# A two-mixer block: xn's transposition, the order of the sums on VectorE, the second tile's row sums, and the norm's root on GpSimd are moved

## The chip, the cores and the metric

The kernel runs on one core of a Trainium2 chip. A core has TensorE (matrix products, written PE, its weight loads PEld), VectorE (DVE), ScalarE (ACT), GpSimd (POOL) and SyncE (SP, which issues DMA transfers). The metric is device time in microseconds (us) from start to end of one execution; lower is better.

## The reference

All data are float32. The input x has shape (4, 1024, 512), 4096 tokens of 512. Four layers follow each other, each with a layer norm ahead and its input added behind:

```python
x = x + attn_a(layernorm(x))   # mixer A: 16 heads of 64, state 64
x = x + ffn(layernorm(x))
x = x + attn_b(layernorm(x))   # mixer B: 64 heads of 16, state 128
x = x + ffn(layernorm(x))
```

A mixer projects the normed input to a gate z (1024 columns), a part xBC, and dt (one column for each head); it runs a causal convolution of four taps over xBC and a SiLU, splits it into x, B and C, and then computes, token by token,

```python
state = state * dA_t + einsum(dtx_t, B_t)
y_t   = einsum(C_t, state)
y     = y + D * x
```

with dt = softplus(dt + dt_bias), dA = exp(dt * A). y is gated with silu(z), normed by its root mean square (in A the gate comes before the norm, in B behind it), and projected back to 512 columns. The feed-forward layer works on a gate for each token and one message for each sequence; the change doesn't touch it.

## The kernel before

The program runs the stages A, F, B, F, one after the other. A mixer stage works on supertiles of 256 tokens, 16 of them, and a supertile has two tiles of 128 tokens, j = 0 and 1. Supertile 0 and the last two are written out, the 13 between run in a hardware loop. The recurrence is done in chunks of one tile: within a tile by products with a matrix of decays (seg, decay, ydiag), between tiles by a state that is carried along (yoff reads it, state0 and state1 add to it).

Each engine runs an order of its own, and they meet in semaphores. TensorE's order is written by `schedule` and `head` as a list of step names. While supertile i is finished, the projections of supertile i + 1 are put between its steps: dt and the blocks blk0, blk1, ... (9 in A, 10 in B) in the first tile's half, z0, z1, z2 in the second's, and z's last quarter, zz, at the start of the next head. The names that matter here:

- zz, z0 to z2, blk, dt: projections with w_in, line 527 (dt at 556). They read xnT.
- xnT0, xnT1: transposition of the normed input xn of supertile i + 1 (line 551), copied by ScalarE (`xnT_copy`, line 738).
- xT0 to xT3, BG (A) or BT, GT (B): transpositions of the convolved x and B, and B times C (lines 571, 576, 533).
- prs, prt, pout: for the last tile of the supertile before, the sums of squares (line 625), the column of them (629), and the projection with w_out (633). rs0, rt0 and out0 are the same for tile 0 of this supertile. VectorE copies the sums (`square_sums`, 1121), forms the variance (`rms_var`, 1125), scales (`out_scale`, 95 to 97) and adds the projection to the residual (`out_add`, 1135).
- yoff0a, yoff0b, yoff1a, yoff1b: products with the state (604 in A, 606 in B), taken by VectorE's `from_state` (1079) into y1. GpSimd then adds the skip part (1291), forms xw from xdt (1302 in A, 1298 in B), and decays the state (1308).
- small0, small1: row sums of the two tiles (595), taken by `small_sums` on VectorE (1049, 1050), from which `exponent_sides` (1059 to 1064) makes the operands of seg.
- make_xdt (1023 in A, 1018 in B): x times dt. slot_mult (1090): the product with gt that makes decay ready for ydiag; two slots a tile in A, eight in B.
- norm_stats, norm_rsqrt and norm_apply: the layer norm of the supertile after the next: statistics on VectorE (928 to 933), the root as exp(-0.5 ln v) on ScalarE (733, 734), refined by one Newton step on VectorE (`newton_rsqrt`, 87 to 90), and applied (940).

All steps that are not seg, ydiag or ident use one of two banks of PSUM, work[0] and work[1], in turns. A step therefore waits until the step two places ahead of it in the list has been taken out of its bank; `freed` says by whom. That is the rule by which an order on one engine becomes a wait on another:

```python
if idx >= 2:
    freed(pe, sec.uses[idx - 2], i, n)
```

For instance, in the head the transposition xnT1 is two places ahead of dt, and pout two places ahead of blk0; pout's bank is free once `out_add` is done.

Of the kernel before, what the change touches and what calls it, by code (L numbers as in the profile page):

```python
# [11 lines left out]
P = 128  # L12
# [72 lines left out]
def newton_rsqrt(dve, nc, link, r, v, tmp):  # L85

    link(nc.vector.tensor_tensor(tmp, r, r, ALU.mult))
    link(nc.vector.tensor_tensor(tmp, tmp, v, ALU.mult))
    link(nc.vector.tensor_scalar(tmp, tmp, -0.5, 1.5, ALU.mult, ALU.add))
    link(nc.vector.tensor_tensor(r, r, tmp, ALU.mult))  # L90


# [7 lines left out]
def build_constants(nc, ctx, ffn):  # L100
# [9 lines left out]
    c["mean_w"] = sb("mean_w", [P, P])  # L110
    c["ident_bf"] = sb("ident_bf", [P, P], BF16)
# [22 lines left out]
    with nc.Block() as block:  # L134
# [12 lines left out]
        def _(pool):  # L147
# [49 lines left out]
def mixer_phase(nc, sig, before, cfg, c, first_mixer, psum, x_src, x_dst, w):  # L197
# [19 lines left out]
    with ctx:  # L217
# [16 lines left out]
        ln_v, ln_r, ln_t = sb("ln_v", [P, 2]), sb("ln_r", [P, 2]), sb("ln_t", [P, 2])  # L234
# [108 lines left out]
        def head(prev, nxt):  # L343
            return (["zz", "xT0", "xT1", "xT2", "xT3"] + b_and_g + ["seg0.0"] + (["prs"] if prev else [])
                    + ["yoff0a", "yoff0b"] + (["prt"] if prev else [])
                    + (["xnT0", "xnT1"] if nxt else []) + (["pout"] if prev else []))

        def schedule(prev, nxt):

            steps = head(prev, nxt)  # L350
            for p in range(NP):
                steps += fill0[2 * p] if nxt else []
                steps += [f"seg0.{p + 1}"] if p + 1 < NP else ["small1"]
# [116 lines left out]
        with nc.Block() as block:  # L470
# [252 lines left out]
            def _(act):  # L723
# [6 lines left out]
                def norm_rsqrt(m):  # L730

                    act.wait_ge(var_ready, m + 1)
                    link(nc.scalar.activation(ln_r[:], ln_v[:], ACT.Ln))
                    nc.scalar.activation(ln_r[:], ln_r[:], ACT.Exp, scale=-0.5).then_inc(r0_ready, 1)

# [98 lines left out]
                def supertile(sec, prev, nxt):  # L834
                    i = sec.i
                    z_copy(sec, "zz")
                    for k in range(4):
                        xt_copy(sec, k)
# [8 lines left out]
                    if nxt:  # L847
                        xnT_copy(sec, 0)
                        xnT_copy(sec, 1)
# [14 lines left out]
                    for p in range(NP):  # L864
# [5 lines left out]
                        if p == 0 and sec.ln is not None:  # L870
                            norm_rsqrt(sec.ln)
# [17 lines left out]
                norm_rsqrt(0)  # L889
# [11 lines left out]
                norm_rsqrt(1)  # L901
# [3 lines left out]
                per = 4  # L905
# [13 lines left out]
            def _(dve):  # L919
# [15 lines left out]
                def norm_apply(n):  # L935
                    dve.wait_ge(r0_ready, n + 1)
                    newton_rsqrt(dve, nc, link, ln_r[:], ln_v[:], ln_t[:])
# [201 lines left out]
                def supertile(sec, prev, nxt):  # L1139
                    i = sec.i  # L1140
                    masked_gt(sec)
                    make_xdt(sec, 0)
# [10 lines left out]
                    if prev:  # L1153
                        out_add(sec, "pout", i - 1, 1)
                    for p in range(NP):
                        for g in (2 * p, 2 * p + 1):
# [11 lines left out]
                            elif g % 2 == 0:  # L1168
                                small_sums(sec, 1)
# [70 lines left out]
                per = 2 + 3 + 3 + 2 + 2 * NB + 2 * 4  # L1240
# [15 lines left out]
            def _(pool):  # L1256
# [7 lines left out]
                def tile_steps(i, j):  # L1264
# [36 lines left out]
                    else:  # L1301
# [628 lines left out]
```

## Time and profile before

| | us |
|---|---|
| median of three runs | 3284.08 |
| lowest, highest | 3274.63, 3286.74 |
| the profiled execution | 3287.7 |
| its span | 3286.0 |
| TensorE busy | 2902.2 |
| VectorE busy | 2016.2 |
| ScalarE busy | 1248.0 |
| GpSimd busy | 875.1 |

Mixer A lasts to about 1310 us of the span, the first feed-forward stage to about 1590, mixer B to about 3030. The mean granted clock of TensorE is 0.938 of full speed. Rows with a start time come from one execution; "idle before" in brackets is how long the engine had nothing to run ahead of a row, and what it then waited for. The ends of matmuls are modelled, and successive ones overlap a little.

### The profile page before, as it was taken

To read this page: it belongs to the slowest core of one execution; us is meant where nothing else is said; L and a number is where in the kernel's file an instruction comes from. 1 tells how busy PE (TensorE), PEld (TensorE's weight loads), DVE (VectorE), ACT (ScalarE), POOL (GpSimd) and SP (SyncE) were. 2 spreads that over 40 slices of the span, in tenths; PEclk is the share of its full clock that TensorE was granted. 3 is DMA by queue.
4 is the path that set the end of the run, shared out by engine and by line. 5 is a ranking of instruction groups with operands and counts; after the bars stand their busy time and mean duration, and the time that the engine had idled before them with its cause. 6 is when DMAs were issued, how large, how long until landed. Compare 5 with 4: busy or idle time off the path is not lost. (4 is left out here: it accounts for less than half of the span.)

```text
span 3286.0 us, 54402 instructions
## 1 busy us (share of the span) xinstructions
PE 2902.2 (88%) x19824; PEld 1887.3 (57%) x19824; DVE 2016.2 (61%) x3825; ACT 1248.0 (38%) x2098; POOL 875.1 (27%) x585
## 2 busy tenths in 40 slices
PE   4989999999999998797599999999999999997896
PEld 3666666666666664344466666666666666664443
DVE  3555555555555554258477777777777777766257
ACT  2343333333333332232244444444444444443232
POOL 0222222222222223134032333232233322223134
PEclk9899999999999999798799999999999999999798
DMA  3000000000000000523300000000000000000523
GB/s 113 14 20 19 19 19 22 22 19 19 19 19 19 19 13 20 224 90 138 115 14 21 13 19 13 19 19 19 19 19 19 13 19 19 13 14 18 220 95 136
DMA packets 80673, 140.15 MB, mean 43 GB/s; under 512 B 18121, under 2 KB 18633, under 8 KB 79569
## 3 DMA queue, kind: packets, MB, share of 16 engines
q1 hardware_dynamic: 60048, 126.29, 10.8%
q10 hardware_dynamic: 20544, 12.79, 1.4%
q8 instruction: 51, 0.84, 0.1%
q14 instruction: 30, 0.24, 0.0%
HBM read 104.98 MB, written 33.55 MB: 42 GB/s over the span
## 5 line engine op out<-in xcount | busy, mean ns | idle before, releaser
L527 PE MATMUL work<-b_xnT,b_w_in 128*128 128x256 f32 x2304 | 549.9, 389 | 25.1 <-DVE b_w_out L1236 9.7
L527 PE MATMUL work<-a_xnT,a_w_in 128*128 128x256 f32 x2176 | 504.9, 388 | 38.2 <-DVE a_parts L1050 21.0
L527 PEld LDWEIGHTS work<-b_xnT,b_w_in 128*128 128x128 f32 x2304 | 426.5, 191 | 112.5 <-ACT b_cv L754 20.3
L527 PEld LDWEIGHTS work<-a_xnT,a_w_in 128*128 128x128 f32 x2176 | 412.0, 193 | 115.3 <-DVE a_parts L1050 27.1
L1090 DVE TENSOR_TENSOR b_decay<-b_decay,b_gt 128x1024 f32<-128x1024 f32 x256 | 331.4, 1326 | 68.2 <-ACT b_decay L806 66.0
L806 ACT ACTIVATE b_decay<-seg 128x1024 f32<-128x1024 f32 x256 | 249.5, 1020 | 162.0 <-PE seg L652 161.2
L633 PE MATMUL work<-a_w_out,a_yz 128*128 128x512 f32 x512 | 275.9, 701 | 18.7 <-ACT a_xnT L738 11.3
L1260 POOL TENSOR_TENSOR rhs<-b_l_side,of_head 128x1024 fp32r<-128x1024 f32 x32 | 63.9, 1996 | 807.7 <-DVE b_l_side L1059 807.7
L633 PE MATMUL work<-b_w_out,b_yz 128*128 128x512 f32 x512 | 248.5, 641 | 30.4 <-ACT b_xnT L738 19.3
L1291 POOL TENSOR_TENSOR a_y<-a_y,a_skip 128x1024 f32<-128x1024 f32 x32 | 102.2, 3193 | 605.2 <-DVE a_y L1079 605.2
L969 DVE SCALAR_TENSOR_TENSOR b_cv<-b_pre,b_conv_w,b_cv 128x256 f32<-128x256 f32 x480 | 224.8, 497 | 55.2 <-ACT b_cv L754 47.3
L969 DVE SCALAR_TENSOR_TENSOR a_cv<-a_pre,a_conv_w,a_cv 128x256 f32<-128x256 f32 x432 | 191.0, 482 | 90.6 <-ACT a_cv L754 84.9
L633 PEld LDWEIGHTS work<-a_w_out,a_yz 128*128 128x128 f32 x512 | 112.9, 227 | 160.2 <-issue 136.5
L633 PEld LDWEIGHTS work<-b_w_out,b_yz 128*128 128x128 f32 x512 | 102.4, 206 | 154.8 <-issue 119.7
L760 ACT COPY a_z_raw<-work 128x512 f32<-128x512 f32 x64 | 37.4, 585 | 300.0 <-PE work L527 300.0
L666 PE MATMUL y<-b_decay,b_xdt 128*32 128x128 f32 x4096 | 142.4, 276 | 2.8 <-DVE b_decay L1090 1.8
L1291 POOL TENSOR_TENSOR b_y<-b_y,b_skip 128x1024 f32<-128x1024 f32 x32 | 88.4, 2763 | 201.8 <-DVE b_y L1079 201.8
L753 ACT COPY b_pre<-work 128x256 f32<-128x256 f32 x160 | 59.8, 374 | 193.1 <-PE work L527 193.1
L666 PEld LDWEIGHTS y<-b_decay,b_xdt 128*32 128x32 f32 x4096 | 102.8, 109 | 49.2 <-issue 34.7
L1478 PE MATMUL y<-f_x1T,f_gate_w 128*128 128x512 f32 x256 | 127.3, 629 | 1.5 <-ACT f_x1T L1603 1.5
L1135 DVE SCALAR_TENSOR_TENSOR a_x_res<-work,a_rr,a_x_res 128x512 f32<-128x512 f32 x32 | 24.0, 751 | 156.4 <-PE work L633 156.4
L753 ACT COPY a_pre<-work 128x256 f32<-128x256 f32 x144 | 53.6, 372 | 173.8 <-PE work L527 173.8
(318 smaller groups left out, 4805.6 us busy)
## 6 DMA issues: line engine op xcount, KB each, us to landing
f_d_w<-in_L_ffn_d_w SPq DMA_DIRECT2D x4, 4096.0 KB, 24.6
f_x_in<-x_mid ACTq DMA_DIRECT2D x12, 1024.0 KB, 6.2
a_x_in<-in_L_attn_a_x SPq DMA_DIRECT2D x16, 512.0 KB, 3.7
a_x_res<-in_L_attn_a_x SPq DMA_DIRECT2D x32, 256.0 KB, 2.7
x_mid<-a_x_res SPq DMA_DIRECT2D x32, 256.0 KB, 2.0
f_x_res<-x_mid SPq DMA_DIRECT2D x8, 1024.0 KB, 6.0
f_bc_w<-x_mid SPq DMA_DIRECT2D x8, 1024.0 KB, 5.6
b_x_in<-x_mid SPq DMA_DIRECT2D x16, 512.0 KB, 3.7
```

Of the source, the lines that this page charges most:

```text
L527: mm = nc.tensor.matmul(dst, w_in[:, k, col:col + m], xnT[:, k, :], start=(k == 0), stop=(k == KD - 1))
L633: mm = nc.tensor.matmul(bank[:, :], yz[:, k, :], w_out[:, k, :], start=(k == 0), stop=(k == KE - 1))
L666: mm = nc.tensor.matmul(ybank[32 * q:32 * q + 32, slot * P:(slot + 1) * P], xdt[:, j, 4 * slot + q, 16 * odd:16 * odd + 32], decay[:, slot ...
L753: nc.scalar.copy(pre[0:m, b, HALO:], bank[0:m, 0:SUP])
L760: nc.scalar.copy(z_raw[:, 2 * k:2 * k + 2, :], sec.bank(name)[:, :].rearrange("p (b t) -> p b t", b=2)).then_inc(z_ready, 1)
L806: nc.scalar.activation(decay[:, slot_buffer(j, s)].rearrange("p h l -> p (h l)"), seg[s % 2][:, :], ACT.Exp).then_inc(exp_done, 1)
L969: ins = nc.vector.scalar_tensor_tensor(out=cv[0:m, b, :], in0=pre[0:m, b, t:t + SUP], scalar=conv_w[0:m, b, t:t + 1], in1=cv[0:m, b, :], o ...
L1090: nc.vector.tensor_tensor(d, d, gt[:, j].unsqueeze(1).to_broadcast([P, 8, P]), ALU.mult).then_inc(m_ready, 1)
L1135: nc.vector.scalar_tensor_tensor(out=x_res[:, j, :], in0=sec.bank(name)[:, :], scalar=rr[:], in1=x_res[:, j, :], op0=ALU.mult, op1=ALU.add ...
L1260: nc.gpsimd.tensor_tensor(c["rhs"][1][:], l_side[:, 1].unsqueeze(1).to_broadcast([P, 8, P]), c["of_head"][:].unsqueeze(2).to_broadcast([P, ...
L1291: nc.gpsimd.tensor_tensor(y1[:], y1[:], skip[:], ALU.add).then_inc(y1x_ready, 1)
L1478: mm = nc.tensor.matmul(ybank[:, (m % 2) * 512:(m % 2 + 1) * 512], gate_w[:, k, m * P:(m + 1) * P], x1T[n][:, k, :], start=(k == 0), stop= ...
```

## The change

It does five things, in both mixers, and renumbers lines by 7 to 18.

1. xnT0 and xnT1 stand directly behind zz in TensorE's list, and ScalarE copies them right behind zz's copy. Before they stood ahead of pout.
2. small1, the second tile's row sums, stands behind pout. Before it stood among the blocks, ahead of the last ydiag steps of tile 0. VectorE takes it with `small_sums(sec, 1)` behind `out_add` of pout; `exponent_sides` stays where it was.
3. VectorE runs the sums of squares and `from_state` first: `make_xdt(sec, 0)` comes behind `rms_var` of prt, and in the second tile `slot_mult(sec, 1, 0)` behind `rms_var` of rt0.
4. The norm's root is one power instruction on GpSimd, behind its last step of the supertile's second tile. The two activations and the Newton step go.
5. GpSimd's loop is peeled by three supertiles, so that its root steps have constant counts at the ends; a constant of -0.5 is made once.

```diff
         def head(prev, nxt):
-            return (["zz", "xT0", "xT1", "xT2", "xT3"] + b_and_g + ["seg0.0"] + (["prs"] if prev else [])
-                    + ["yoff0a", "yoff0b"] + (["prt"] if prev else [])
-                    + (["xnT0", "xnT1"] if nxt else []) + (["pout"] if prev else []))
+            return (["zz"] + (["xnT0", "xnT1"] if nxt else []) + ["xT0", "xT1", "xT2", "xT3"] + b_and_g + ["seg0.0"]
+                    + (["prs"] if prev else []) + ["yoff0a", "yoff0b"] + (["prt", "pout"] if prev else []) + ["small1"])
...
-                steps += [f"seg0.{p + 1}"] if p + 1 < NP else ["small1"]
+                steps += [f"seg0.{p + 1}"] if p + 1 < NP else []
...
 # ScalarE, supertile
                     z_copy(sec, "zz")
+                    if nxt:
+                        xnT_copy(sec, 0)
+                        xnT_copy(sec, 1)
                     for k in range(4):
                         xt_copy(sec, k)
...
                     slot_exp(sec, 0, 1)
-                    if nxt:
-                        xnT_copy(sec, 0)
-                        xnT_copy(sec, 1)
...
-                        if p == 0 and sec.ln is not None:
-                            norm_rsqrt(sec.ln)
...
 # VectorE
                 def norm_apply(n):
                     dve.wait_ge(r0_ready, n + 1)
-                    newton_rsqrt(dve, nc, link, ln_r[:], ln_v[:], ln_t[:])
...
                     masked_gt(sec)
-                    make_xdt(sec, 0)
                     if prev:
                         square_sums(sec, "prs")
                     from_state(sec, 0)
                     if prev:
                         rms_var(sec, "prt")
+                    make_xdt(sec, 0)
                     slot_mult(sec, 0, 0)
...
                         out_add(sec, "pout", i - 1, 1)
+                    small_sums(sec, 1)
...
                             elif g % 2 == 0:
-                                small_sums(sec, 1)
                                 exponent_sides(2 * i + 1)
...
                     state_add(sec, 0)
-                    slot_mult(sec, 1, 0)
                     square_sums(sec, "rs0")
                     from_state(sec, 1)
+                    rms_var(sec, "rt0")
+                    slot_mult(sec, 1, 0)
                     slot_mult(sec, 1, 1)
-                    rms_var(sec, "rt0")
                     out_scale(2 * i)
...
 # GpSimd
+                def norm_rsqrt(m):
+                    pool.wait_ge(var_ready, m + 1)
+                    nc.gpsimd.tensor_tensor(ln_r[:], ln_v[:], c["root"][:], ALU.pow).then_inc(r0_ready, 1)
...
+                tile_steps(0, 0)
+                tile_steps(0, 1, ln=2)
+                with pool.Fori(0, NSUP - 3) as r:
+                    tile_steps(r + 1, 0)
+                    tile_steps(r + 1, 1, ln=r + 3)
```

What this does to the order on the engines is shown at three places. First TensorE, the head of the last supertile of A but one, from zz (line 527, after the change 520) to the first projections of the next. L551 and 544 are xnT, L571 and 564 xT, L633 and 626 pout, L595 and 588 small1, L556 and 549 dt. Before:

```order
L527 MATMUL work<-a_xnT,a_w_in 128x256 x8
L571 MATMUL work<-ident,a_xs 128x128 x16
...
L625 MATMUL work<-a_sq,ones 32x128 x8
L604 MATMUL work<-a_state,a_bcs 128x512 x2
L629 MATMUL work<-quad_row,a_rs 128x1
L551 MATMUL work<-ident,a_xn 128x128 x8
L633 MATMUL work<-a_w_out,a_yz 128x512 x8
L556 MATMUL work<-a_w_in,a_xnT 128x16 x8
```

And now:

```order
L520 MATMUL work<-a_xnT,a_w_in 128x256 x8
L544 MATMUL work<-ident,a_xn 128x128 x8
L564 MATMUL work<-ident,a_xs 128x128 x16
...
L618 MATMUL work<-a_sq,ones 32x128 x8
L597 MATMUL work<-a_state,a_bcs 128x512 x2
L622 MATMUL work<-quad_row,a_rs 128x1
L626 MATMUL work<-a_w_out,a_yz 128x512 x8
L588 MATMUL work<-tri_le,a_aa 64x128 x2
L549 MATMUL work<-a_w_in,a_xnT 128x16 x8
```

The transposition moved ahead of xs, and the row sums moved in between pout and dt, so that pout is now two places ahead of dt.

Second VectorE, the same head. L1023 and 1005 are xdt, L1121 and 1103 the copy of the sums, L1090 and 1072 the slot products, L1135 and 1117 the addition of pout. Before:

```order
L1040 TENSOR_TENSOR a_gt<-work,tri_le 128x256
L1023 TENSOR_TENSOR a_xdt<-a_xt,a_dt 128x1024
L1121 COPY a_rs<-work 128x128
L1079 TENSOR_TENSOR a_y<-work,a_e 128x512 x2
L1125 TENSOR_SCALAR a_rv<-work 128x1
L1090 TENSOR_TENSOR a_decay<-a_decay,a_gt 128x1024
```

And now:

```order
L1022 TENSOR_TENSOR a_gt<-work,tri_le 128x256
L1103 COPY a_rs<-work 128x128
L1061 TENSOR_TENSOR a_y<-work,a_e 128x512 x2
L1107 TENSOR_SCALAR a_rv<-work 128x1
L1005 TENSOR_TENSOR a_xdt<-a_xt,a_dt 128x1024
L1072 TENSOR_TENSOR a_decay<-a_decay,a_gt 128x1024
```

xdt of tile 0 moved from ahead of the sums to behind the variance.

Third VectorE at the second tile, from the addition to the state (L1098, now 1080) on. Before:

```order
L1098 TENSOR_TENSOR a_state<-a_state,work 128x512
L1090 TENSOR_TENSOR a_decay<-a_decay,a_gt 128x1024
L1121 COPY a_rs<-work 128x128
L1079 TENSOR_TENSOR a_y<-work,a_e 128x512 x2
L1090 TENSOR_TENSOR a_decay<-a_decay,a_gt 128x1024
L1125 TENSOR_SCALAR a_rv<-work 128x1
```

And now:

```order
L1080 TENSOR_TENSOR a_state<-a_state,work 128x512
L1103 COPY a_rs<-work 128x128
L1061 TENSOR_TENSOR a_y<-work,a_e 128x512 x2
L1107 TENSOR_SCALAR a_rv<-work 128x1
L1072 TENSOR_TENSOR a_decay<-a_decay,a_gt 128x1024 x2
```

The slot products moved behind the copy of the sums, the state part and the variance.

## Rows read from the trace of the kernel before

**Rows 1.** page of the profile, part 1: busy time, share of the span, instructions
```profile
PE 2902.2 (88%) x19824; PEld 1887.3 (57%) x19824; DVE 2016.2 (61%) x3825; ACT 1248.0 (38%) x2098; POOL 875.1 (27%) x585
```

**Rows 2.** timeline of SyncE's queue (start us, us, what): reload of x in mixer B
```profile
1714.09 0.40 SPq L490 DMA_DIRECT2D b_x_in<-x_mid  x1
...
1801.56 0.39 SPq L490 DMA_DIRECT2D b_x_in<-x_mid  x1
...
2775.49 0.38 SPq L490 DMA_DIRECT2D b_x_in<-x_mid  x1
```

**Rows 3.** timeline of mixer A, TensorE (in brackets idle before): second tile's sums, out0
```profile
600.63 0.64 PE L625 MATMUL work<-a_sq,ones 128*32 128x128 f32 x16
...
603.37 1.12 PE L604 MATMUL work<-a_state,a_bcs 64*128 64x512 f32 x2 [1.04 <-DVE a_rs L1121]
...
605.28 8.59 PE L633 MATMUL work<-a_w_out,a_yz 128*128 128x512 f32 x16 [0.47 <-DVE a_y L1079]
```

**Rows 4.** window of the same out0 (us, busy of each engine, granted clock, DMA)
```profile
604.85:608.25 3.40, 2.97 (x4) 1.43 (x5) 2.21 (x6) 0.41 (x2) 2.87 (x1) 0.50 0.00 0
```

**Rows 5.** timeline of mixer B, TensorE: head of a supertile
```profile
2253.27 0.60 PE L571 MATMUL work<-ident,b_xs 128*128 128x128 f32 x4
...
2256.78 0.71 PE L533 MATMUL work<-b_bcs 128*128 128x128 f32 x4
...
2258.34 0.64 PE L625 MATMUL work<-b_sq,ones 128*32 128x128 f32 x16
...
2261.76 1.09 PE L551 MATMUL work<-ident,b_xn 128*128 128x128 f32 x8 [0.37 <-DVE b_y L1079]
...
2264.24 7.13 PE L633 MATMUL work<-b_w_out,b_yz 128*128 128x512 f32 x16 [1.39 <-ACT b_xnT L738]
...
2271.21 1.89 PE L556 MATMUL work<-b_w_in,b_xnT 128*128 128x64 f32 x16
```

**Rows 6.** timeline, TensorE: row sums of the second tile (L595), mixers A and B
```profile
580.94 0.44 PE L595 MATMUL work<-tri_le,a_aa 128*64 128x128 f32 x4
...
585.34 7.17 PE L527 MATMUL work<-a_xnT,a_w_in 128*128 128x256 f32 x32 [1.40 <-DVE a_parts L1050]
...
2206.75 0.61 PE L595 MATMUL work<-tri_le,b_aa 128*128 128x128 f32 x4
...
2212.24 1.08 PE L666 MATMUL y<-b_decay,b_xdt 128*32 128x128 f32 x32
```

**Rows 7.** timeline of the head in rows 5: GpSimd and VectorE
```profile
2261.79 2.35 POOL L1291 TENSOR_TENSOR b_y<-b_y,b_skip 128x1024 f32<-128x1024 f32 x1 [4.38 <-DVE b_y L1079]
...
2262.54 2.68 DVE L1090 TENSOR_TENSOR b_decay<-b_decay,b_gt 128x1024 f32<-128x1024 f32 x1 [0.84 <-ACT b_decay L806]
...
2267.16 3.90 DVE L1018 TENSOR_TENSOR b_xdt<-b_xt,b_dt 128x512 f32<-128x512 f32 x2
```

**Rows 8.** one line's instructions: duration in ns, least, median, most
```profile
L1090 DVE TENSOR_TENSOR b_decay<-b_decay,b_gt x256: 1207/1219/3244, 1648.5 to 3017.5; 128x1024 f32<-128x1024 f32 x128
...
L1018 DVE TENSOR_TENSOR b_xdt<-b_xt,b_dt x64: 679/1120/2420, 1645.2 to 2978.5; 128x512 f32<-128x512 f32 x64
...
L1298 POOL TENSOR_TENSOR b_xw<-b_xdt,b_e x64: 1064/1560/2062, 1650.7 to 3005.4; 128x512 f32<-128x512 f32 x64
...
L1291 POOL TENSOR_TENSOR b_y<-b_y,b_skip x32: 2346/2762/3181, 1648.4 to 3001.2; 128x1024 f32<-128x1024 f32 x32
...
L1308 POOL TENSOR_TENSOR b_state<-b_state,b_e x32: 1930/2097/2264, 1654.8 to 3006.6; 128x1024 f32<-128x1024 f32 x32
...
L1856 POOL TENSOR_TENSOR f_m_r<-f_m_v,f_root x8: 1006/1006/1012, 1338.1 to 3132.3; 128x4 f32<-128x4 f32 x8
```

**Rows 9.** timeline of mixer A, TensorE: head of a supertile
```profile
629.88 0.60 PE L571 MATMUL work<-ident,a_xs 128*128 128x128 f32 x4
...
640.10 1.09 PE L551 MATMUL work<-ident,a_xn 128*128 128x128 f32 x8 [0.29 <-DVE a_y L1079]
...
650.66 1.85 PE L556 MATMUL work<-a_w_in,a_xnT 128*128 128x16 f32 x16
```

More of the change, by code:

```diff
@@ L82, in __init__ @@
         self.proj = self.dt_col + heads
[L85 to L90, printed above, removed]
 def newton_rsqrt_column(nc, link, r, v, tmp):
@@ L110, in build_constants @@
     c["mean_w"] = sb("mean_w", [P, P])
+    c["root"] = sb("root", [P, 2])
     c["ident_bf"] = sb("ident_bf", [P, P], BF16)
@@ L157, in _ @@
                 step(nc.gpsimd.memset(c[t][:], v))
+            step(nc.gpsimd.memset(c["root"][:], -0.5))
             for t in (hd, low, lrow):
@@ L233, in mixer_phase @@
         mv = sb("mv", [P, 2, 2])
-        ln_v, ln_r, ln_t = sb("ln_v", [P, 2]), sb("ln_r", [P, 2]), sb("ln_t", [P, 2])
+        ln_v, ln_r = sb("ln_v", [P, 2]), sb("ln_r", [P, 2])
         xn = sb("xn", [P, 2, DM])
@@ L728, in link @@
                     act.wait_ge(a_chain, steps.next())
[L730 to L734, printed above, removed]
                 def xnT_copy(sec, j):
@@ L888, in _ @@
                 sec = prologue()
-                norm_rsqrt(0)
                 act.wait_ge(setup_v, 1)
@@ L900, in _ @@
                     z_copy(sec, f"z{k}")
-                norm_rsqrt(1)
                 sums_exp(0)
@@ L904, in _ @@
                 supertile(first(), False, True)
-                per = 4
+                per = 3
                 base = steps.section(0)
@@ L1239, in _ @@
                 base = steps.section(0)
-                per = 2 + 3 + 3 + 2 + 2 * NB + 2 * 4
+                per = 2 + 3 + 3 + 2 + 2 * NB + 4
                 with dve.Fori(0, NSUP - 3) as r:
@@ L1262, in second_rhs, with tile_steps @@
                                             ).then_inc(rhs_ready[1], 1)
-                def tile_steps(i, j):
+                def norm_rsqrt(m):
+                    pool.wait_ge(var_ready, m + 1)
+                    nc.gpsimd.tensor_tensor(ln_r[:], ln_v[:], c["root"][:], ALU.pow).then_inc(r0_ready, 1)
+                def tile_steps(i, j, ln=None):
                     tile = 2 * i + j
@@ L1310, in tile_steps @@
                                             ).then_inc(dec_done, 1)
+                    if ln is not None:
+                        norm_rsqrt(ln)
                 for s in (skip_done, y1x_ready, dec_done, kept, xw_ready, folded):
                     pool.sem_inc(s, FREE)
+                norm_rsqrt(0)
+                norm_rsqrt(1)
                 pool.wait_ge(small_loaded, 16 * 6)
-                with pool.Fori(0, NSUP) as i:
+                tile_steps(0, 0)
[3 more added lines that the diff above has]
+                    tile_steps(r + 1, 1, ln=r + 3)
+                for i in (NSUP - 2, NSUP - 1):
                     tile_steps(i, 0)
```

## The prediction

> **What bounds the kernel now.** I read the page first, then the idle time of TensorE by releaser, then the timeline of one supertile of each mixer. TensorE is busy 88% of the span and no other engine over 61% [rows 1]; the two feed-forward stages are not touched. So the question for every edit is whether it shortens TensorE's own sequence, idle gaps included. Within a supertile each engine runs a fixed order, so a late step on VectorE becomes a TensorE gap wherever TensorE waits for a bank that this step frees. One pass of mixer B takes 87.47 us (the first in rows 2), the mean of twelve is 88.45 us (2775.49 - 1714.09, by 12) [rows 2]; I take the difference of 1.0 us for the clock. What the clock costs is seen in mixer A: in the first 3.4 us of out0 the granted clock is 0.50, the lower of the two levels, 1.2 GHz [rows 4], after a stretch with little dense work, and the projection takes 8.59 us [rows 3] where the same sixteen rows take 7.13 us at full clock in B [rows 5]. A stretch at half clock under dense work costs about 1.5 to 1.7 us.
>
> **Part 1, sums of squares and state part first (second tile).** Before, the bank copy (line 1121) stood behind a 1.2 us slot product, and the second state matmul waited 1.04 us for it. From the squares' matmuls to out0 it is 605.28 - 600.63 = 4.65 us [rows 3]. The head of B shows the same chain with VectorE free when the sums end: from the squares' matmuls at 2258.34 to the next one behind the root's column at 2261.76 is 3.42 us [rows 5]. After the change the second tile has that order. Gain 1.23 us, 32 times (16 supertiles, two mixers): **-39 us**. The slot products go later by some 2 us; out0's 7 us hide that.
>
> **Part 2, second tile's row sums (small1).** In A, from their start at 580.94 to the next-but-one block at 585.34 is 4.40 us, in which one block is projected; four blocks take 7.17 us, one 1.8 [rows 6]. Without them 2.6 us go. In B 2212.24 - 2206.75 = 5.49 us hold two blocks, 3.6: 1.9 us go [rows 6]. Fifteen supertiles of each mixer have projections there: -39 and -28, **-67 us**. Their own 0.4 to 0.6 us now lie directly behind pout; part 4 shows that TensorE is waiting there.
>
> **Part 3, xn's transposition behind z's last quarter.** Two banks more go through the pair of work banks before xs. In B five steps from bank to bank take 2256.78 - 2253.27 = 3.51 us [rows 5], 0.70 us each, paced by ScalarE's copies; so two more banks put all that follows in the head back by 1.4 us. In return pout need no longer wait for ScalarE to copy xn, and takes the place at which xn was transposed: 2261.76 + 1.4 = 2263.2 instead of 2264.24 [rows 5], a gain of 1.1 us for pout itself.
>
> **Part 4, what that does to VectorE, and who waits.** xdt of the first tile moves from idle time ahead of the sums to behind them, among the work that shares memory with GpSimd. There a slot product that takes 1.21 us alone takes 2.68 us next to GpSimd's addition, and the pair of xdt products 3.90 us [rows 7] where twice 0.68 is the least [rows 8]. So I add both engines' work up, from GpSimd's start of y1: y1 2.35, xw 2 x 1.06, state 1.93, two slot products 2.4, xdt of tile 1 1.36, together 10.2 us [rows 8]; measured were 2267.16 + 3.90 - 2261.79 = 9.27 us [rows 7], so 0.9 overlap. With xdt of tile 0 it is 11.5 - 0.9 = 10.6 us. Counted from the first transposition of xs (2253.27), GpSimd starts at +8.5, after the change at +9.9, and VectorE is done at +20.5. The final addition (out_add) comes then, 0.75 us, and now **dt's projection waits for it**: dt's second-last bank is pout's, before it was xn's. dt starts at about +21.5. Before it was 2271.21 - 2253.27 = +17.9 [rows 5], +18.9 on the mean of the passes [rows 2]. That is 2.6 us later than the mean, 3.5 if nothing overlaps; I take 2.8, 14 times: **+39 us** in B. Behind this gap stand, on TensorE, all blocks of the next supertile.
>
> In B pout ends at +17.0 and the row sums at +17.6, so TensorE idles 3.9 us in B. No row shows such a gap in this place; the bounds are 0 (the 1.39 us ahead of pout kept the clock in rows 5) and one stretch as in rows 4 or two, 3.4 us. I take one stretch, 1.7 us: **+24 us**. In A, xs to the end of the state sums is 640.10 - 629.88 = 10.2, with the shift 11.6 [rows 9]; the work to the end of xdt of tile 1 is 1.36 + 2.35 + 1.21 + 2.13 + 1.21 + 1.36 = 9.6 by B's rows, 8.7 with the overlap, or 9.7 if the decay of the state goes before (half of 1.93, for half the columns) [rows 8]. dt is at +21.3 to +22.3 instead of 650.66 - 629.88 = +20.8. If this head keeps its clock, up to 1.7 less (10.2 against B's 8.5). I take +0.5: **+7 us**. The gap in A is 1.0 us with pout at 8.6 us and 2.5 us with pout at 7.1; half of the passes lose a stretch: **+12 us**. In out0 of A the shorter sums save half of the stretches of 1.5 us: **-11 us**.
>
> What the two engines do to each other is seen in rows 7: the slot product was in progress over the end of GpSimd's addition (2264.14) and ended 1.08 us after it, about as long as it takes alone. The Trainium skill, SBUF — State Buffer, section "SBUF: two separate sides", says that VectorE and GpSimd share one pair of ports as an exclusive lock, held for the whole instruction while the other blocks; the trace agrees in direction, but by the rule the 10.2 us should not fit into 9.27, and the sum would end at the 3267 us of rival (a).
>
> **Part 5, the norm's root on GpSimd.** Two activations and four small VectorE steps become one instruction on GpSimd, which has nothing to do there until the next tile. The mixers have no such instruction; the nearest is the feed-forward's root on twice the columns, 1.01 us [rows 8]. xn is needed only behind z2 and zz, two blocks each, 3.6 us by rows 6, so over 7 us later; those hide it and what VectorE saves: 0, between -1 (VectorE's steps at the full) and 0 per pass; if GpSimd were over 6 us late, the excess would count. SyncE's next load of x comes about 1 us sooner and meets nothing. Constants and first root: under 1 us once.
>
> **Sum.** -39 - 67 + 39 + 24 + 7 + 12 - 11 = -35 us. The profiled execution took 3287.7 us with a span of 3286.0; the median of three is 3284.1, so I subtract from that: **3249 us**.
>
> **Rivals.**
> (a) Strict serial work: the whole 10.2 and 11.5 us without overlap. B loses 0.6 us more than taken, A 0.7: 14 x 1.3 = 18 us. 3267 us. For it speak the 2.68 us in rows 7, against it the 9.27. The rule of SBUF — State Buffer in the Trainium skill, named above, would come out here.
> (b) VectorE is not late: xdt slips into gaps, and out_add waits only for pout. Then in B dt starts at 9.9 + 7.1 + 1.1 = +18.1, 0.8 sooner than the mean, and nothing is lost to the clock there: -11 instead of +39 + 24, in A also no clock loss. -39 - 67 - 11 + 7 - 11 = -121: 3163 us. Against it: VectorE ended xdt at 2267.16 + 3.90 = 2271.06 and pout at 2264.24 + 7.13 = 2271.37 [rows 5, 7]; it had 0.3 us to spare, and has more to do now.
> (c) A gives half of its gain back. A's sum is -20 - 39 + 7 + 12 - 11 = -51; for it speaks that the clock does fall in A behind a gap of the size that parts 3 and 4 now make [rows 3, 4], against it that out0's own gap shrinks. 3274 us.
> (d) Slower: the late out_add. In B the delay is 3.9 us (contention as long as the 3.24 us of the longest slot product in rows 8) and the clock is low for two stretches, 3.4 us; in A 1.4 and 1.7. 14 x (7.3 + 3.1) = 146 against the 106 us of parts 1 and 2: +40, 3324 us. It decides from 7.6 us lost per pair of heads; I have taken 5.9, less 0.8 for out0's clock.
> (e) The order doesn't do what it says: excluded, both engines' orders show the moved steps.
>
> **Numbers.** Forecast 0.42, (a) 0.10, (b) 0.10, (c) 0.20, (d) 0.18. Half a per cent is 16 us, about what a measurement of this kernel can tell from no change: faster is below 3267.7, slower above 3300.5. (a) lies on the edge and is halved: faster 0.42 + 0.10 + 0.05 = 0.57, same 0.25, slower 0.18. Range: leave out (b) and the upper half of (d): 3212 to 3312. The lower end is the forecast with no clock lost behind pout (-36).
>
> **What would show it.** In the profile after: (1) in the second tile the squares' matmuls to out0 in 3.4 us, no wait for the bank copy; (2) no row sums between blocks, blocks at an even 1.8 us; (3) pout about 1.1 us earlier against xs in B; (4) dt behind out_add, TensorE idle 3 to 4 us ahead of it in B and 1 to 2.5 in A, xdt next to y1; (5) the granted clock at 0.50 behind this gap in B. I am wrong if out_add waits for pout in B, if the gap exceeds 5 us, or if the mean granted clock changes by over 0.02.

## The result, and the profile after

The changed kernel takes **3242.4 us** (median of 4 runs, 3235.9 to 3248.2) against 3285.4 us before (median of 4), a ratio of 0.9876 with a 95% interval of 0.9847 to 0.9904: 43 us faster. The forecast was 3249 us. The profiled execution is the fastest of the four and has a span of 3234.2 us (before 3286.0) and a mean granted clock of 0.941 (before 0.938).

From the page of the profile after, part 1, to be held against [rows 1]; TensorE's busy time falls by 37 us, VectorE's rises by 64, GpSimd's by 92. Of GpSimd's 92, 36 are the 32 roots that it has now; the rest, and VectorE's, goes with longer times of the same instructions: a pair of xdt products in B takes 3.75 us on the mean instead of 2.67, an xw in B 1.78 instead of 1.56.

```profile
PE 2865.6 (89%) x19824; PEld 1901.7 (59%) x19824; DVE 2080.6 (64%) x3697; ACT 1246.0 (39%) x2034; POOL 967.3 (30%) x618
```

SyncE's queue in the timeline of after: the fourth and the sixteenth reload of x in mixer A, then the same two in mixer B:

```profile
140.52 0.41 SPq L483 DMA_DIRECT2D a_x_in<-in_L_attn_a_x  x1
...
1033.41 0.38 SPq L483 DMA_DIRECT2D a_x_in<-in_L_attn_a_x  x1
...
1644.20 0.40 SPq L483 DMA_DIRECT2D b_x_in<-x_mid  x1
...
2725.21 0.38 SPq L483 DMA_DIRECT2D b_x_in<-x_mid  x1
```

Twelve passes lie between the two reloads of a mixer: (1033.41 - 140.52) / 12 = 74.41 us in A, where before had 78.34, and 90.08 us in B, where before had 88.45 [rows 2]. **A gained 3.9 us a pass and B lost 1.6.** By stage: from A's first load of x to its last -58 us, from there to B's first -12 (nearly all of it A's last supertiles: A's last projection ends at 1241.2 us instead of 1309.7, 68 us sooner), B's loads +19, the rest -2; together the 52 us of the spans. All kernels below are read by the two pass times.

The second tile in A, timeline of TensorE after [rows 3]:

```profile
646.81 0.64 PE L618 MATMUL work<-a_sq,ones 128*32 128x128 f32 x16
647.38 1.60 PE L597 MATMUL work<-a_state,a_bcs 64*128 64x512 f32 x4
...
649.88 7.13 PE L626 MATMUL work<-a_w_out,a_yz 128*128 128x512 f32 x16 [0.21 <-DVE a_y L1061]
```

From the squares to out0 it is 3.07 us, before 4.65; the wait of 1.04 us for the bank copy is gone, the state part runs in one piece of four, and out0 takes 7.13 us instead of 8.59.

The head in B, timeline of TensorE after [rows 5]:

```profile
2199.82 0.60 PE L544 MATMUL work<-ident,b_xn 128*128 128x128 f32 x4
...
2206.35 0.65 PE L618 MATMUL work<-b_sq,ones 128*32 128x128 f32 x16
...
2209.69 7.13 PE L626 MATMUL work<-b_w_out,b_yz 128*128 128x512 f32 x16 [0.23 <-DVE b_y L1061]
2216.66 0.61 PE L588 MATMUL work<-tri_le,b_aa 128*128 128x128 f32 x4
2220.89 2.16 PE L549 MATMUL work<-b_w_in,b_xnT 128*128 128x64 f32 x16 [3.63 <-DVE b_x_res L1117]
```

Counted from the end of z's last quarter, as the prediction does, pout starts at +9.87 us and dt at +21.07. Ahead of dt TensorE waits 3.63 us for out_add (L1117). The same head on GpSimd and VectorE [rows 7]:

```profile
2209.79 2.87 POOL L1277 TENSOR_TENSOR b_y<-b_y,b_skip 128x1024 f32<-128x1024 f32 x1 [4.44 <-DVE b_y L1061]
...
2209.76 3.46 DVE L1000 TENSOR_TENSOR b_xdt<-b_xt,b_dt 128x512 f32<-128x512 f32 x2
...
2216.29 3.90 DVE L1000 TENSOR_TENSOR b_xdt<-b_xt,b_dt 128x512 f32<-128x512 f32 x2
2220.11 0.74 DVE L1117 SCALAR_TENSOR_TENSOR b_x_res<-work,b_rr,b_x_res 128x512 f32<-128x512 f32 x1
```

The moved xdt of the first tile starts beside GpSimd's addition and takes 3.46 us; VectorE is done with the second at 2220.19 and goes to out_add without a pause, though pout had ended at 2216.8. The list of waits of TensorE after (what it waited for, us in total, times, longest) shows that it is so in each pass, in A by 1.8 us on the mean:

```profile
PE work L549 <- DVE b_x_res L1117: 50.6, 14, 3.6
...
PE work L549 <- DVE a_x_res L1117: 25.6, 14, 2.6
```

Behind the gap the granted clock (third number from the right) falls, as in [rows 4]. Windows of 3.4 us of the same head, after:

```profile
2216.40:2219.80 3.40, 0.87 (x5) 0.44 (x4) 3.40 (x2) 0.00 (x0) 3.16 (x2) 1.00 0.00 0
2219.80:2223.20 3.40, 2.31 (x20) 2.19 (x20) 2.03 (x5) 0.00 (x0) 0.00 (x0) 0.91 0.20 77
2223.20:2226.60 3.40, 3.40 (x27) 2.21 (x28) 2.42 (x7) 2.56 (x4) 0.00 (x0) 0.59 0.22 77
2226.60:2230.00 3.40, 3.40 (x48) 2.83 (x47) 2.93 (x5) 0.84 (x2) 0.00 (x0) 1.00 0.00 0
```

3.4 x (0.09 + 0.41) = 1.7 us of full-speed time are missing. They lie in one piece, at the lower of the two levels throughout:

```profile
2222.63:2226.03 3.40, 3.40 (x27) 2.18 (x27) 1.96 (x7) 2.19 (x4) 0.00 (x0) 0.50 0.22 77
```

This is one of B's shortest passes, 88.8 us; others take 90.4 and 91.8, in steps of the same size.

### The profile page after: what moved, and what is told of

The parts are those of the page before. It is cut to its first block and busy times, and to the rows that moved or that the text cites. A ratio compares the mean times of both kernels' runs of the same rounds, so it can differ in the third digit from the quotient of the medians.

```text
span 3234.2 us, 54113 instructions
## 1 busy us (share of the span) xinstructions
PE 2865.6 (89%) x19824; PEld 1901.7 (59%) x19824; DVE 2080.6 (64%) x3697; ACT 1246.0 (39%) x2034; POOL 967.3 (30%) x618
## 5 line engine op out<-in xcount | busy, mean ns | idle before, releaser
L520 PE MATMUL work<-b_xnT,b_w_in 128*128 128x256 f32 x2304 | 560.5, 398 | 16.5 <-DVE b_parts L1032 8.5
L520 PEld LDWEIGHTS work<-b_xnT,b_w_in 128*128 128x128 f32 x2304 | 441.7, 197 | 103.4 <-issue 16.9
L520 PEld LDWEIGHTS work<-a_xnT,a_w_in 128*128 128x128 f32 x2176 | 421.2, 196 | 86.8 <-issue 12.3
L951 DVE SCALAR_TENSOR_TENSOR b_cv<-b_pre,b_conv_w,b_cv 128x256 f32<-128x256 f32 x480 | 249.6, 548 | 85.5 <-ACT b_cv L741 77.5
L1242 POOL TENSOR_TENSOR rhs<-b_l_side,of_head 128x1024 fp32r<-128x1024 f32 x32 | 82.0, 2564 | 648.5 <-DVE b_l_side L1041 648.5
L626 PE MATMUL work<-a_w_out,a_yz 128*128 128x512 f32 x512 | 241.0, 626 | 5.4 <-DVE a_y L1061 5.4
L626 PE MATMUL work<-b_w_out,b_yz 128*128 128x512 f32 x512 | 228.3, 599 | 11.6 <-DVE b_y L1061 11.6
L626 PEld LDWEIGHTS work<-a_w_out,a_yz 128*128 128x128 f32 x512 | 99.5, 200 | 123.1 <-issue 115.0
L1072 DVE TENSOR_TENSOR a_decay<-a_decay,a_gt 128x1024 f32<-128x1024 f32 x64 | 148.2, 2338 | 0.8 <-ACT a_decay L793 0.3
L1277 POOL TENSOR_TENSOR b_y<-b_y,b_skip 128x1024 f32<-128x1024 f32 x32 | 97.7, 3052 | 165.4 <-DVE b_y L1061 165.4
L1271 POOL TENSOR_TENSOR a_skip<-a_xt,a_d_skip 128x1024 f32<-128x1024 f32 x32 | 76.5, 2391 | 160.6 <-ACT a_xt L774 160.6
```

Source lines behind the costliest of these rows:

```text
L520: mm = nc.tensor.matmul(dst, w_in[:, k, col:col + m], xnT[:, k, :], start=(k == 0), stop=(k == KD - 1))
L626: mm = nc.tensor.matmul(bank[:, :], yz[:, k, :], w_out[:, k, :], start=(k == 0), stop=(k == KE - 1))
L951: ins = nc.vector.scalar_tensor_tensor(out=cv[0:m, b, :], in0=pre[0:m, b, t:t + SUP], scalar=conv_w[0:m, b, t:t + 1], in1=cv[0:m, b, :], o ...
L1072: nc.vector.tensor_tensor(d, d, gt[:, j].unsqueeze(1).to_broadcast([P, 8, P]), ALU.mult).then_inc(m_ready, 1)
L1242: nc.gpsimd.tensor_tensor(c["rhs"][1][:], l_side[:, 1].unsqueeze(1).to_broadcast([P, 8, P]), c["of_head"][:].unsqueeze(2).to_broadcast([P, ...
L1271: nc.gpsimd.tensor_tensor(skip[:].rearrange("p (h q) -> p h q", h=H), xt[:, j, :].rearrange("p (h q) -> p h q", h=H), d_skip[:].unsqueeze( ...
```

## Experiments

Ratios are to the kernel before, timed on the same chip. Pass: mean of twelve passes in A and B. Wait: mean wait for out_add in each head, on dt where nothing else is said. Low: how long the granted clock stood at its lower level, 0.50, in a mean of the same twelve passes; at half the clock, at most half of that time is lost.

| kernel | median us | ratio, 95% interval | pass A / B, us | wait A / B, us | low A / B, us |
|---|---|---|---|---|---|
| before | 3285.4, 3283.5, 3283.0 | | 78.34 / 88.45 | none | 9.7 / 2.3 |
| after | 3242.4 | 0.9876 [0.9847, 0.9904] | 74.41 / 90.08 | 1.8 / 3.6 | 6.8 / 6.3 |
| sums_first | 3199.1 | 0.9742 [0.9726, 0.9758] | 74.87 / 86.62 | none | 5.4 / 1.1 |
| small1_moved | 3218.5 | 0.9801 [0.9787, 0.9814] | 75.33 / 87.48 | 0.5 / 0.4 | 7.7 / 2.0 |
| xn_moved | 3229.2 | 0.9833 [0.9820, 0.9847] | 76.37 / 87.24 | first block, 0.3 / 0.5 | 6.0 / 0.9 |
| root_moved | 3260.6 | 0.9925 [0.9911, 0.9938] | 78.31 / 87.43 | none | 9.7 / 0.9 |
| xdt_back | 3220.9 | 0.9815 [0.9801, 0.9829] | 74.86 / 88.76 | 1.0 / 2.5 | 9.4 / 5.7 |
| xdt_first | 3217.1 | 0.9800 [0.9787, 0.9814] | 74.86 / 88.76 | 1.0 / 2.5 | 9.4 / 5.7 |
| xdt1_late | 3121.8 | 0.9506 [0.9490, 0.9522] | 71.97 / 84.06 | 0.6 / 0.4 | 4.0 / 0 |
| both_xdt | 3109.6 | 0.9475 [0.9462, 0.9488] | 71.63 / 84.06 | 0.5 / 0.4 | 3.4 / 0 |
| small1_back | 3206.4 | 0.9765 [0.9750, 0.9780] | 74.71 / 87.09 | first block, 1.3 / 1.6 | 4.0 / 1.7 |
| gap_filled | 3206.0 | 0.9763 [0.9743, 0.9784] | 75.11 / 87.28 | 2.2 / filled | 7.4 / 0 |
| y_short | 3153.3 | 0.9603 [0.9586, 0.9620] | 71.69 / 86.58 | 0.6 / 1.6 | 3.4 / 2.8 |
| dt_ahead | 3091.5 | 0.9417 [0.9402, 0.9432] | 71.57 / 83.45 | none | 5.4 / 0 |

### One part of the change alone, on the kernel before

The parts carry the prediction's numbers. What its part 4 is about, the first tile's late xdt on VectorE, has no run of its own here; xdt_back, further down, is the changed kernel without it, and so the other four together.

**sums_first**, part 1:

```
-slot_mult(sec, 1, 0)
 square_sums(sec, "rs0")
 from_state(sec, 1)
-slot_mult(sec, 1, 1)
 rms_var(sec, "rt0")
+slot_mult(sec, 1, 0)
+slot_mult(sec, 1, 1)
```

> The kernel before with part 1 alone: in the second tile VectorE copies the squares' sums and makes y1 and the mean before its first slot product. Theory (each part acts as its own step of the sum says): squares to out0 falls from 4.65 to between 3.42 us and the 3.07 us that the changed kernel shows in A, 32 times, so -39 to -51 us, and a few us less clock loss in A's out0; ratio about 0.985 (3230 to 3246 us). Rival (VectorE only moves its lateness): the slot products end 2 us later and the blocks or the row sums behind out0 wait for it, half of the gain returns, ratio 0.993 (3258 to 3268 us).

It brought 86 us, more than the theory's best. The gap is as expected, 3.08 us from squares to out0 in A. The rest is clock. In A the pass is 3.5 us shorter: 1.6 from the gap and 1.46 from out0, 7.13 us where it took 8.59. Timeline of TensorE, A:

```profile
576.39 0.65 PE L625 MATMUL work<-a_sq,ones 128*32 128x128 f32 x16
...
579.47 7.13 PE L633 MATMUL work<-a_w_out,a_yz 128*128 128x512 f32 x16 [0.21 <-DVE a_y L1079]
```

**small1_moved**, part 2: the row sums at the end of the head on TensorE, small_sums behind out_add on VectorE.

> The kernel before with part 2 alone: the second tile's row sums directly behind pout, all else as before; dt's second-last bank is then pout's, so dt waits for out_add here too. Theory: 2.6 us go in each of 15 supertiles of A and 1.9 in B (-67 us), and dt starts 0.7 to 1.9 us later behind out_add, 14 times in each mixer (+20 to +50 us); between them about -30 us, ratio 0.985 to 0.997 (3235 to 3275 us). Rival (the sums between the blocks hid VectorE's work on them, so nothing is gained and the wait for out_add is all that is left): 0 to +30 us, ratio 1.000 to 1.009.

67 us, and both theories fell: the 67 us of part 2 came in full, but the 20 to 50 us of waiting that the theory set against them did not. The wait for out_add is 0.5 and 0.4 us while pout stands where it did before.

**xn_moved**, part 3: xn's two transpositions and copies behind z's last quarter.

> The kernel before with part 3 alone: xn's transposition behind z's last quarter, xdt of the first tile still ahead of the sums, row sums still among the blocks. dt's second-last bank is the mean's, so dt doesn't wait for out_add. Theory: pout and dt 1.1 us sooner in B (-15 us), dt 0.5 to 1 us later in A (+7 to +14 us), together -10 to 0, ratio 0.997 to 1.000 (3274 to 3286 us). Rival (the four xs transpositions behind it make ScalarE late for all that follows, 1.4 us in each head with nothing given back): +40 us, ratio 1.012.

Both theories fell: 56 us, of which 30 are A's (2.0 us a pass) and 18 B's. Timeline of TensorE, A, to be held against [rows 9]:

```profile
620.57 0.60 PE L571 MATMUL work<-ident,a_xs 128*128 128x128 f32 x4
...
629.32 7.13 PE L633 MATMUL work<-a_w_out,a_yz 128*128 128x512 f32 x16 [0.21 <-DVE a_y L1079]
636.29 1.85 PE L556 MATMUL work<-a_w_in,a_xnT 128*128 128x16 f32 x16
```

From the first transposition of xs to dt it is 15.72 us, 17.1 with the 1.4 that xn's now takes ahead of it, and 20.78 in [rows 9]. The wait for ScalarE's copy of xn ahead of pout is gone, and with it a low clock: in this pass the head ran at full clock, and pout took 7.13 us where it took 8.83. The head does so in ten of A's twelve passes, but some of them lose clock in out0 instead (up to 10.2 us), so that A's mean pass gains 2.0 us and not 3.7.

**root_moved**, part 5: the root as one instruction on GpSimd.

> The kernel before with part 5 alone: the norm's root as one instruction on GpSimd. Theory: 0, ratio 0.999 to 1.001 (within 3 us), because xn is needed seven or more us later. Rival (part 5 is where A's surplus over the sum comes from: four VectorE steps and two activations fewer behind out0, over 1 us per pass): -15 to -30 us, ratio 0.991 to 0.995.

25 us, by neither theory's way. A's passes are equal. The first out0 of A comes 6.5 us sooner (128.63 us instead of 135.14), and it is the one-off start that did it: before the first supertile VectorE waited for the second root, which stood in ScalarE's queue behind the copies of the blocks and of z, and only then scaled w_out. Timeline of VectorE, before:

```profile
72.70 0.16 DVE L87 TENSOR_TENSOR a_ln_t<-a_ln_r 128x2 f32<-128x2 f32 x1 [5.67 <-ACT a_ln_r L734]
...
77.02 3.24 DVE L1236 TENSOR_SCALAR a_w_out<-a_w_out,a_norm_w 128x512 f32<-128x512 f32 x8
```

and with the root on GpSimd:

```profile
65.43 1.00 DVE L923 TENSOR_SCALAR a_xn<-a_x_in,a_mv,a_ln_r 128x512 f32<-128x512 f32 x2 [0.81 <-POOL a_ln_r L1249]
...
72.87 3.25 DVE L1219 TENSOR_SCALAR a_w_out<-a_w_out,a_norm_w 128x512 f32<-128x512 f32 x8
```

TensorE's first z behind w_out starts at 76.17 us instead of 80.32. Of these 4.15 us, 2.4 were there before that root was asked for (its variance is made at 64.44 us instead of 66.87), so 1.7 us go with the wait; where the others come from is not shown. In B the pass is 1.0 us shorter on the mean: three of its twelve passes take 88.7 us and nine 87.0 to 87.1, where before has eight of 88.8 to 89.1 and four of 87.4. So 0.4 us is in every pass and the rest is a stretch of low clock in fewer of them; what moves it is open.

The four parts alone sum to 86 + 67 + 56 + 25 = **234 us; the whole change brought 43**. The next runs look for the other 191.

### What holds dt back

**xdt_back**: the changed kernel, the first tile's xdt where it was.

```
 masked_gt(sec)
+make_xdt(sec, 0)
 ...
     rms_var(sec, "prt")
-make_xdt(sec, 0)
 slot_mult(sec, 0, 0)
```

> The changed kernel with one line moved back: VectorE makes the first tile's xdt behind the masked product and ahead of the squares' sums, as before. Theory S (the four parts that were timed alone add up to 234 us, the whole brought 43; the missing 190 us are the price of this one line, by out_add's lateness and the clock behind it): TensorE's wait for out_add ahead of dt falls from 3.6 us in B and 1.8 in A to about 0.5; ratio to before 0.93 to 0.945 (3055 to 3105 us). Rival R (serial work on the shared memory: the line gives back only its own 1.4 us per head): out_add 1.0 to 1.4 us sooner, 14 times in B, less in A, ratio 0.979 to 0.984 (3217 to 3232 us). Rival O (the parts overlap: each alone saves the same stretch of low clock): ratio 0.955 to 0.975.

Theories S and O fell, R held: 21 us, the wait in B 2.5 instead of 3.6. The line costs about its own length in B, 1.3 us a pass; in A the wait is 0.8 us shorter but the pass is not (74.86 us against 74.41), with 9.4 us of low clock instead of 6.8. The lateness of out_add was there without it. This kernel is the four parts together: **63 us, of 234 singly**. So 20 of the 191 us are the late xdt, and 171 are lost between the four parts.

**xdt_first**: the same line ahead of masked_gt.

> The changed kernel with the first tile's xdt ahead of the masked product, in VectorE's longest idle stretch of the head (7.0 us in A, 4.9 in B). Theories S and R as for the other place; in addition the copy of the squares' sums is not put back by the 0.3 us that xdt would end behind their matmuls in B: 0 to 10 us under the kernel with xdt behind the masked product. Rival (xt comes too late, so that the masked product and all behind it is late): 10 us or more over it.

As fast as xdt_back, 3.8 us apart by medians and with intervals that overlap; the passes are the same.

**xdt1_late**: the first xdt stays where the change put it; the second goes behind out_add.

```
-make_xdt(sec, 1)
 if prev:
     out_add(sec, "pout", i - 1, 1)
 small_sums(sec, 1)
 ...
         dt_raw(sec)
+        make_xdt(sec, 1)
+        dve.wait_ge(xdt_done, FREE + 2 * i + 2)
         dt_finish(sec)
```

> The changed kernel with the second tile's xdt on VectorE behind out_add, the row sums and the first read of dt's bank, the first tile's where the change put it. out_add then waits for pout alone. Theory (dt's wait for out_add is the loss): the wait falls from 3.6 us to under 1.5 in B and from 1.8 to under 1 in A, low clock behind it goes in B; ratio 0.955 to 0.972 (3138 to 3193 us). Rival (VectorE's serial work is the loss and only moves to the convolutions and blocks behind): ratio 0.980 to 0.990.

**121 us less than the changed kernel, more than the theory's best.** Nothing is left out of VectorE's work; 3.9 us of it in B and 2.1 in A only no longer stand ahead of out_add. Behind it, with GpSimd no longer at work beside them, the same products take 1.4 and 1.2 us. Waits of TensorE:

```profile
PE work L549 <- DVE a_x_res L1117: 8.2, 14, 0.7
...
PE work L549 <- DVE b_x_res L1117: 5.7, 14, 0.5
```

In B the pass is 6.0 us shorter, of which the wait is 3.2, and the granted clock never falls. In A it is 2.4 shorter, of which the wait is 1.2.

**both_xdt**: both edits.

> The changed kernel with both: the first tile's xdt ahead of the masked product, the second's behind out_add and the first read of dt's bank. Theory: dt waits only for pout and out_add, 0.9 us; as fast as the faster of the two single edits, within 10 us. Rival: the later second xdt puts softplus, the convolutions and so the next supertile's decays back, 10 us or more over the kernel with the first edit alone.

12 us under xdt1_late; B is the same to the hundredth, A 0.3 us a pass shorter. The medians are a little over the 10 us that the theory gave it.

### Why the wait costs more than its length, and what fills it

**gap_filled**: in B four matmuls between the row sums and dt.

```
+if name == "dt" and PADDED and "pout" in sec.uses:
+    for k in range(4):
+        nc.tensor.matmul(ybank[:, 0:512], w_out[:, k, 0:P], w_out[:, k, :], start=True, stop=True)
 use(name, sec)
```

> The changed kernel with four matmuls of 128 x 512 on TensorE between the row sums and dt in B's head (3.6 us of work whose result is thrown away: it lands in the y bank, which is written anew later). dt still starts when out_add is done; what goes is only the idle time. Theory C (behind the gap B loses time to the lower clock, one stretch of 1.7 us by the prediction, 2.8 us by the passes: 90.1 against 84.1 us where the wait is gone, less 3.2 for the wait itself): granted clock 0.99 to 1.00 in B, passes 87.3 to 88.4 us, ratio to before 0.973 to 0.981. Rival (the work behind the gap is slow for another reason, or the filler is simply added): passes of 90 us or more, ratio 0.985 to 1.000.

Theory C held. Timeline of TensorE, then the windows of the head:

```profile
2208.53 3.60 PE L689 MATMUL y<-b_w_out 128*128 128x512 f32 x8
2212.32 2.00 PE L549 MATMUL work<-b_w_in,b_xnT 128*128 128x64 f32 x16 [0.19 <-DVE b_x_res L1121]
```

```profile
2207.90:2211.30 3.40, 3.40 (x12) 1.78 (x11) 3.40 (x2) 0.00 (x0) 3.08 (x2) 1.00 0.00 0
2211.30:2214.70 3.40, 3.21 (x27) 2.07 (x25) 2.15 (x6) 0.00 (x0) 0.00 (x0) 1.00 0.20 77
2214.70:2218.10 3.40, 3.40 (x48) 2.79 (x48) 2.46 (x6) 3.06 (x6) 0.00 (x0) 1.00 0.21 77
```

dt still starts when out_add is done, and **with 3.6 us more of work per pass B is 2.8 us a pass faster** (87.28 against 90.08), all twelve passes alike to 0.2 us; over these passes the granted clock is 1.00, in the changed kernel 0.97. That is the price of the clock. The other 3.2 us to xdt1_late's 84.06 are the wait itself. A's code is as in the changed kernel, yet its mean pass is 0.7 us longer in this execution (75.11 against 74.41): differences of a few tenths in A's passes are not to be read.

**y_short**: GpSimd's addition of skip to y1 on 64 of 1024 columns.

> The changed kernel with GpSimd's addition of skip to y1 on 64 of 1024 columns; the rest of y's skip term is left out. Theory (VectorE and GpSimd add up on the shared memory): the first xdt products take 1.4 to 2.0 us instead of 3.46 in B, out_add comes about 2.2 us sooner, the wait ahead of dt falls from 3.6 to about 1.4 in B and from 1.8 to under 0.8 in A; ratio to before 0.960 to 0.972 (3153 to 3192 us). Rival (xdt is slow by its own strides and the wait is VectorE's own work): wait over 3 us, ratio 0.983 to 0.988.

The theory held. VectorE in B's head:

```profile
2235.41 1.42 DVE L1000 TENSOR_TENSOR b_xdt<-b_xt,b_dt 128x512 f32<-128x512 f32 x2
...
2239.90 3.90 DVE L1000 TENSOR_TENSOR b_xdt<-b_xt,b_dt 128x512 f32<-128x512 f32 x2
```

The same pair of products takes 1.42 us instead of 3.46 when GpSimd has 0.83 us of work beside it instead of 2.87; the second pair, still next to xw and the state's decay, takes 3.90 as before. All of the 2.04 us arrive at dt: the wait falls from 3.6 to 1.6.

**small1_back**: the changed kernel without part 2.

> The changed kernel without part 2: the second tile's row sums back among the blocks, the rest as changed, the late first xdt too. dt's second-last bank is then the mean's, and dt follows pout directly; out_add is still late and is waited for one bank later, ahead of the first block, with dt's 2.0 us as cover. Theory (the wait for out_add and the clock behind it come only with the row sums in that place): gap 3.6 to about 1.5 us in B and none in A, clock kept in B; B's passes 86 to 88 us instead of 90.1, A's 75 to 76 instead of 74.4; ratio to before 0.970 to 0.985 (3186 to 3236 us). Rival (VectorE's lateness costs the same wherever it is met): part 2's 67 us are lost, ratio 1.005 to 1.010.

The theory held in B and in the sum, in A neither for the wait nor for the pass (74.7 us, 75 to 76 expected): 36 us faster than the whole change, though part 2 alone is worth 67. With the row sums back among the blocks dt doesn't wait; the first block does, 1.6 us in B behind dt's 2.0, and 1.3 in A in ten passes, where none was expected. The clock is not always kept: B's passes take 86.2 or 87.9 us.

### A faster kernel

**dt_ahead**: both_xdt, and on TensorE dt ahead of the row sums.

```
-... + (["prt", "pout"] if prev else []) + ["small1"])
+... + (["prt", "pout"] if prev else []))
 ...
-steps += fill0[2 * p] if nxt else []
+first = fill0[2 * p] if nxt else []
+steps += first[:1] + ["small1"] + first[1:] if p == 0 else first
```

> The kernel with both xdt moved (3110 us) and on TensorE dt ahead of the row sums, so that dt's second-last bank is the mean's and out_add has dt's 2.0 us as cover; on VectorE the row sums are copied behind dt's first read. Theory (what is left in the heads is a wait of 0.4 to 0.5 us for out_add and a low clock in A's blocks behind it): 0.5 us less in each pass of B, 0.5 to 1.0 in A; 3085 to 3102 us, ratio 0.940 to 0.945. Rival (the first block now waits for VectorE's copy of dt and the row sums): 3110 to 3140 us.

**3091 us, 5.8% under the kernel before and 4.7% under the changed one.** B's passes are 0.6 us shorter, as expected; A's only 0.1, less than expected: its wait of 0.5 us is gone, but the clock is low for 5.4 us a pass instead of 3.4. dt now lies over out_add, and no wait for it is in the list. Largest wait left in A's passes: the squares' matmuls for ScalarE's squares, 0.94 us, and the clock falls in that stretch (0.58 in a window of 3.4 us).

```profile
586.80:590.20 3.40, 2.98 (x20) 1.59 (x20) 0.29 (x1) 3.37 (x4) 0.00 (x0) 0.58 0.00 0
```

## Why the prediction was right, point by point

- **Part 1, -39:** the step was 3.42 us and is 3.07 in A, 3.35 in B, so 1.58 and 1.30 saved: -46. The slot products behind it are hidden, as forecast, but for some 2 us in all of B.
- **Part 2, -67:** alone it brought 67, with its own small wait for out_add in it; the 1.0 and 0.3 us less of low clock that the run also shows are not in the sum. In the changed kernel the blocks run in one piece, without a gap.
- **Part 3:** pout comes 1.1 us sooner in B (+9.87 against +10.97), as worked out. That in A the head would keep its clock (up to 1.7 less) was named and given almost nothing; alone, A's clock is about half of part 3's 56 us (low for 6.0 us a pass instead of 9.7).
- **Part 4, VectorE and GpSimd added up:** from GpSimd's start to the end of the second xdt 10.6 us were forecast, 2220.19 - 2209.79 = 10.4 measured. dt at +21.07 against +21.5: 2.2 us late instead of 2.8, +30 instead of +39. The mean of +18.9 for before holds: pout took 8.6 to 8.8 us in seven of the twelve heads. The head in rows 5, from which the prediction takes it that a gap of 1.39 us keeps the clock, is one of the five others: in the seven, the same gap did not keep it.
- **Part 4, the clock in B, +24:** the mechanism was right and the size too small. One stretch of 1.7 us was taken; 2.8 us a pass were measured by filling the gap, 14 times: +39. The two errors go against each other: +63 forecast, +69 measured. Sign 5 came: one stretch at 0.50 in the head shown, one to three in others.
- **Part 4 in A:** the gap is 2.6 us in half of the passes, where pout took 7.13 us, and 0.5 or 1.1 in the others, where pout took 8.7 to 9.8; forecast were 2.5 and 1.0. Behind each of the long ones follows a stretch of low clock, so "half of the passes" came as well. Passes are 3.9 us shorter, 3.4 forecast (51 / 15).
- **Out0's clock in A, -11:** the kind was right and the size half. Before, out0 took 8.5 us or more in all 16 supertiles, after 7.13 in all 16: 1.46 us each, -23.
- **Part 5, 0:** right in A's loop (78.31 us alone, against 78.34). In B's loop it is 1.0 us a pass alone, at the edge of the -1 to 0 that was given, and partly clock. Wrong at the start: "under 1 us once" missed that the roots of the start stood in ScalarE's queue, and that w_out's scaling on VectorE waited behind one. A's first out0 comes 6.5 us sooner; 1.7 of them are shown to be that wait.
- **Rivals:** (a) doesn't hold, 10.4 us is below the 11.5 of serial work; the Trainium skill, SBUF — State Buffer, section "SBUF: two separate sides", has it that the pair of ports goes to one engine for the whole instruction, and y_short agrees with it in size (2.04 us less beside 2.04 us less of GpSimd), the sum of the head only to within 1.1 us. (b) was excluded by the 3.63 us wait. Its case, out_add waiting for pout alone, is what xdt1_late makes, and its price of -121 us was too low for it: -162. (c) and (d): A gained more than forecast, and B's heads lost 2.2 + 2.8 = 5.0 us, so that with a gaining A the 7.6 from which (d) decides were not reached.

So the mechanism was as forecast, and the total was right with some luck. In the profiled execution A's last projection ends 68 us sooner, where 51 were forecast (about 12 of the difference are out0's clock, the rest is the start), and the time from there to B's last is 18 us longer, where 15 were forecast. That makes 52 us with the rest, 17 more than the forecast; by the medians it is 43 against 35.

What the prediction did not see is how much more the parts were worth: 234 us singly, of which the whole lost 191. Of these, 20 are the late first xdt (xdt_back), and 121 are shown to hang on out_add behind the second xdt (xdt1_late). It seems to take parts 2 and 3 together to make out_add the bound: part 3 brings pout forward to where VectorE is not done, part 2 puts the row sums between, so that dt's second-last bank is pout's. Without part 2 dt does not wait (small1_back); with part 2 alone it waits 0.5 us (small1_moved), with all four parts 2.5 in B (xdt_back). That it is part 3 that makes this difference is argued from the earlier pout: no run has parts 2 and 3 without 1 and 5.

Some 70 us remain between xdt1_late and the sum of the parts; its passes are 0.6 us over the sum of the single gains in B, 2.1 in A. The column of low clock shows why they could not add up. Before, the clock is low for 9.7 us a pass in A and 2.3 in B. The four parts alone take 4.3, 2.0, 3.7 and 0 us of it away in A, together 10.0, and 1.2, 0.3, 1.4 and 1.4 in B, together 4.3: more than there was. xdt1_late took 5.7 and 2.3. At half cost, the 4.3 us missing in A are about 2.1 us, as much as its passes are over; the 2.0 missing in B are at most 1.0, and its passes are 0.6 over. The same stretches of low clock are saved by more than one part, and can be saved only once.

## What to carry to other kernels

Ask of each instruction of a secondary engine who waits for what stands behind it: the same products on VectorE (3.9 us in B, 2.1 in A) cost 121 us ahead of the addition that frees a bank; behind it no wait for them is left in B's passes, and its clock never falls. Cost a gap of the matmul engine with the clock that it loses, which here came to nearly as much again as the gap. Parts of a change that each gain alone may meet in one new wait; time them singly and then look at the wait that only the whole has.

## What was unexpected on the hardware

- Work whose result is thrown away made the kernel faster: 3.6 us of matmuls in a gap of 3.6 us gave 2.8 us back per pass (gap_filled, 0.9763 against 0.9876).
- Behind a gap of 1.6 us in the same place (y_short) passes of B took 85.2, 86.8 or 88.4 us, steps of 1.6: the same code loses the clock for no, one or two stretches.
- VectorE's and GpSimd's times are not their own: the same pair of products took 1.42 us beside a short GpSimd instruction and 3.46 beside a long one.
- The same holds for GpSimd's power on 128 x 2: 0.71 us in A, where VectorE stands idle until it is done, and 1.64 us in B's loop, where it starts 0.15 us behind a slot product on VectorE and ends about 0.6 us after that one.
